# Layer 0: sums of squares dealt out by a transfer, the norms' key bias as a column of the keys, and its offset in one VectorE operation per kind

## The reference

```python
q = _ln(q, qln_w, qln_b)
k = _ln(k, kln_w, kln_b)
...
qx = _ln(qx, qxln_w, qxln_b)
kx = _ln(kx.reshape(b, sc, g, d), kxln_w, kxln_b)
...
core = _gqa(q, k, v).reshape(b, s, nh * d)
xout = _gqa(qx, kx, vx).reshape(b, s, nh * d)
cat = jnp.concatenate([core, xout], axis=-1)
catq = _div_clamp_fp8(cat, proj_smooth)
```

## Time and profile before

| | us |
|---|---|
| median of 3 runs | 1788.65 |
| lowest, highest | 1786.4, 1791.87 |
| span of the profiled execution | 1787.7 |

### The profile page before, as it was taken

How to read it: one execution, slowest core, us unless ns; L and a number is a source line. 1 busy time by engine, 2 the same in 40 slices (tenths; PEclk the granted TensorE clock), 3 DMA queues, 4 the chain that set the end, 5 groups by cost and what they waited for, 6 DMA issues and landing times. The chain is left out here.

```text
span 1787.7 us, 44278 instructions
## 1 busy us (share of the span) xinstructions
PE 1631.5 (91%) x16245; PEld 1038.3 (58%) x16438; DVE 1474.9 (83%) x3476; ACT 1386.3 (78%) x2365; POOL 1367.9 (77%) x1171
## 2 busy tenths in 40 slices
PE   3389999999999999999999999997898999999997
PEld 1256776777767767777777777765454333333332
DVE  8889999999999989999999999998896765645422
ACT  4287887888878777887887888775234999999996
POOL 3557787887878888888888888887897998979500
PEclk8599999999999999999999999999899999999999
DMA  4268999999899979999999999998523222222100
GB/s 168 93 130 180 184 187 193 198 194 190 189 199 184 200 150 198 191 231 184 195 195 192 217 213 190 194 186 160 171 42 110 41 44 75 43 37 43 31 14 13
DMA packets 603176, 261.42 MB, mean 146 GB/s; under 512 B 568784, under 2 KB 575952, under 8 KB 601552
## 3 DMA queue, kind: packets, MB, share of 16 engines
q1 hardware_dynamic: 602960, 258.57, 70.1%
HBM read 99.15 MB, written 17.28 MB: 65 GB/s over the span
## 5 line engine op out<-in xcount | busy, mean ns | idle before, releaser
L1800 PE MATMUL pv<-PT,VV 128*128 128x256 bf16 (+1 forms) x2880 | 340.9, 275 | 9.2 <-DMA PT<-PB 9.2
L1780 PE MATMUL score<-KK,QT 128*128 128x512 bf16 (+2 forms) x1795 | 315.6, 318 | 32.6 <-DVE mxp L1249 24.3
L2370 POOL TENSOR_TENSOR l_rr<-l_rr,mhalf 128x32 f32<-128x32 f32 (+1 forms) x60 | 332.8, 5546 | 5.0
L1521 ACT ACTIVATE PB<-S,rsum 128x1024 bf16<-128x1024 f32 (+1 forms) x256 | 246.2, 988 | 105.3 <-DVE rsum L1281 101.1
L1800 PEld LDWEIGHTS pv<-PT,VV 128*128 128x128 bf16 (+1 forms) x2880 | 280.7, 99 | 76.4 <-issue 35.2
L1272 DVE SCALAR_TENSOR_TENSOR PB<-S,rsum,PB 128x1024 bf16<-128x1024 f32 (+1 forms) x256 | 318.7, 1246 | 2.7 <-ACT PB L1521 2.6
L1780 PEld LDWEIGHTS score<-KK,QT 128*128 128x128 bf16 x1920 | 159.9, 98 | 164.5 <-DVE mxp L1249 32.3
L1511 ACT ACTIVATE S<-S,nmx 128x1601 f32<-128x1601 f32 x128 | 209.7, 1638 | 28.3 <-DVE nmx L1263 27.8
L2636 ACT ACTIVATE P<-score 128x1024 f32<-128x1024 f32 x196 | 199.4, 1063 | 12.7 <-PE score L2728 6.0
L1076 POOL TENSOR_SCALAR S<-S,rsum 128x256 f32<-128x256 f32 x128 | 122.0, 954 | 86.1 <-DVE rsum L1281 86.1
L2748 PE MATMUL pv<-P,V 128*9 128x256 f32 (+1 forms) x2288 | 153.9, 384 | 3.8 <-DVE pv L2174 2.4
(11 more groups left out here) (275 smaller groups left out, 3686.7 us busy)
## 6 DMA issues: line engine op xcount, KB each, us to landing
x<-rs_d SPq DMA_DIRECT2D x16, 936.0 KB, 7.6
rsb<-rs_d SPq DMA_DIRECT2D x16, 936.0 KB, 6.0
wsb<-w_split SPq DMA_DIRECT2D x46, 256.0 KB, 4.7
wsb<-w_split SPq DMA_DIRECT2D x23, 512.0 KB, 5.2
wpr<-in_wprojT SPq DMA_DIRECT2D x23, 512.0 KB, 3.9
context_d<-stage SPq DMA_DIRECT2D x16, 400.2 KB, 3.7
l_ctx<-context_d SPq DMA_DIRECT2D x4, 1601.0 KB, 8.1
rawh<-in_w_all SPq DMA_DIRECT2D x12, 512.0 KB, 5.6
```

Source lines behind the costliest of these rows:

```text
L1521: e.activation(m.PB[n % 2][:, 2 * a:a + b], m.S32[n % 2][:, a:b], ACT.Copy, scale=m.rsum[n % 2][:, 1:2]).then_inc(s["p_hi"], 1)
L1780: i = e.matmul(m.score[:, at:at + b - a], qt[:, kind, qp, q * P:(q + 1) * P], kk[:, kp, a:b], start=(k == 0), stop=(k == 2))
L1800: i = e.matmul(m.pv[:, at:at + 256], vv[0:rows, v, t, :], m.PT[k % 2][0:rows, turned(c, a), :], start=(c == first and r == 0), stop=(c == ...
L2370: e.tensor_tensor(rr, rr, m.mhalf[0:rows, 0:NH1], ALU.pow).then_inc(s["l1_rr"], 1)
```

## The change

The four rows of sums (now 480 wide) are copied by ACT with the epsilon added, and a transfer from SBUF to SBUF (`turn_sums`) deals them out to 128 partitions of 15. GpSimd takes the power of a 128x15 tile, and `row_out` writes that tile as it is to `rs_d`. The two sorts of PE transposes, VectorE's `squares_out` and ACT's `norms_out` go, and with them the slot ST (left empty) and RS. The key bias over sqrt(128) becomes one more column of each kind of keys (high and low part), written by VectorE in the first two turns alone, so that the scores' matmuls are 66 and 257 columns wide for 65 and 256 and bring q.b along in `m.score`. The eight matmuls, `m.kb` and `cb` go. `offset` becomes one scalar_tensor_tensor per kind, with q.b read from PSUM. Since it reads PSUM, `scores(n, 1)` now waits for `negmax` of the tile before. On GpSimd `key_norm` moves behind `split_self(4*it + 1)`. A few small tiles move in SBUF.

```diff
-SQG, SQT = 4, 4
-SQW = (KC + SQG * SQT - 1) // (SQG * SQT)
+SQG = 4
+SQC = (KC + P - 1) // P
+SQW = P * SQC // SQG
...
-         ("V2",), ("RS", "V3"), ("PR",))
+SLOTS = (("Q0",), ("K0",), ("K1",), ("TQ0",), ("K2",), ("K3",), ("Q1",), ("SS",), ("V0",), (), ("V1",), ("TQ1",), ("V2",),
+         ("V3",), ("PR",))
...
+    def turn_sums(it):
+        e.wait_ge(s["sums_out"], it + 1)
+        if it:
+            e.wait_ge(s["kr_pow"], it)
+        e.dma_start(m.ssc[:, :], m.sqs[0:SQG * R:R, :].rearrange("j (r c) -> j r c", c=SQC)).then_inc(s["sums_in"], 16)
...
     def row_out(it):
-        e.wait_ge(s["rst_out"], it + 1)
+        e.wait_ge(s["kr_pow"], it + 1)
...
-        e.dma_start(m.rs_d[it % 2], m.rsr[0:SQN, 0:SQW]).then_inc(s["rs_row"], 16)
+        e.dma_start(m.rs_d[it % 2], m.rr[:, :]).then_inc(s["rs_row"], 16)
...
     def key_norm(it):
-        e.wait_ge(s["ssq_out"], it + 1)
+        e.wait_ge(s["sums_in"], 16 * (it + 1))
...
+        e.tensor_tensor(m.rr[:, :], m.ssc[:, :], m.mhalf[:, 0:SQC], ALU.pow).then_inc(s["kr_pow"], 1)
...
+        split_self(4 * it + 1)
         key_norm(it + 1)
         if it == -1:
             pool_round_end(e, m, s, 5)
-        split_self(4 * it + 1)
...
     def offset(n):
-        e.tensor_tensor(m.mxc[par][:, :], m.mx[par][:, :], c, ALU.add).then_inc(s["maxed"], 1)
-        e.wait_ge(s["maxed"], n + 1)
         if n >= 2:
             e.wait_ge(s["exp_s"], n - 1)
-        e.tensor_tensor(m.nmx[par][:, :], c, m.mxc[par][:, :], ALU.subtract).then_inc(s["negmax"], 1)
+        for kind in range(2):
+            c, top = m.score[:, BIAS[kind]:BIAS[kind] + 1], m.mx[par][:, kind:kind + 1]
+            i = e.scalar_tensor_tensor(m.nmx[par][:, kind:kind + 1], top, c, c, ALU.add, ALU.subtract, reverse1=True)
+        i.then_inc(s["negmax"], 1)
...
-        e.copy(m.sqs[:, :], bank_of(m, "SS")[:, 0:SQT * SQW]).then_inc(s["sums_out"], 1)
+        e.activation(m.sqs[:, :], bank_of(m, "SS")[:, 0:SQW], ACT.Copy, bias=D * EPS5).then_inc(s["sums_out"], 1)
...
-        if n:
-            e.wait_ge(s["mm"], 3 * (n - 1) + (1, 3)[half])
+        if n and half == 0:
+            e.wait_ge(s["mm"], 3 * (n - 1) + 1)
+        elif n:
+            e.wait_ge(s["negmax"], n)
...
-            (1, 1024, 1536, 1024), (1, 1536, SC, 1536), (0, SC, KC, SELF0))
+            (1, 1024, 1536, 1024), (1, 1536, SC + 1, 1536), (0, SC + 1, KCOLS, SELF0))
```

More of the change, by code:

```diff
@@ L29 @@
 KC = SC + S
+KCOLS = KC + 2
 KTILES = KT + TB
@@ L894, in wait_bank @@
         it, at = it - 1, at + len(SLOTS)
-    if SLOTS[at] == ("PR",) and 0 <= it < LAG:
+    if not SLOTS[at] or SLOTS[at] == ("PR",) and 0 <= it < LAG:
         at -= 3
@@ L1655, in squares @@
         if it == 0:
-            e.wait_ge(s["p_pad"], 2)
-        w = SQT * SQW
+            e.wait_ge(s["p_pad"], 1)
         for j in range(SQG):
-            r = e.matmul(bank[j * R:(j + 1) * R, 0:w], m.ones[:, :], m.sq[:, j * w:(j + 1) * w], start=True, stop=True,
-                         skip_group_check=True)
-        r.then_inc(s["pa_full"], 1)
-    def turn_squares(it):
-        if not it < NGB:
-            return
-        bank = bank_of(m, "ST")
-        wait_bank(e, s, it, "ST")
-        e.wait_ge(s["sums_out"], it + 1)
-        for t in range(SQT):
-            r = e.transpose(bank[0:SQW, t * P:(t + 1) * P], m.sqs[:, t * SQW:(t + 1) * SQW], m.ident[:, :])
+            r = e.matmul(bank[j * R:(j + 1) * R, 0:SQW], m.ones[:, :], m.sq[:, j * SQW:(j + 1) * SQW], start=True,
+                         stop=True, skip_group_check=True)
         r.then_inc(s["pa_full"], 1)
@@ L1698, in values @@
                              start=(n == 0), stop=(n == 3))
-            e.wait_ge(s["q_hi"], 2 * it + 2)
-            for kind, q in itertools.product(range(2), range(NQ)):
-                at = 3 * D + kind * NQ + q
-                e.matmul(bank[:, at:at + 1], m.QT[it % 2][:, kind, 0, q * P:(q + 1) * P], m.kb[:, kind:kind + 1],
-                         start=True, stop=True)
             for n, (ic, part, w) in enumerate(inner):
```

117 lines of the change are left out of this document (39 added, 78 removed).

## The result

The changed kernel takes **1831.2 us** (median; 1827.0 to 1832.72, four runs) against 1787.53 for the kernel before in the same runs: a ratio of 1.0236, interval 1.0211 to 1.026. It is 44 us slower. I had forecast 24 us faster, and the time lies outside the range.

A forecast was written before the change was run, and what follows sets the result against it. PE was taken to bound the second part (35.0 us a turn), a PE-VectorE ring the first (36.9), the norms' row close behind. Gains 18 + 5 + 1 = 24 us; 1787.7 - 24 + 0.95 = 1764.6, range 1747 to 1790.

The forecast's parts named there:

- PE in the second part: Last 15 measured turns of layer 0's loop: PE's instruction stream sets the pace, 35.0 us a turn, falling to 34.0.
- the ring: First 15 measured turns: PE from released scores to values, then VectorE to `mxp`; 36.9 us a turn, 1.2 saved.
- The two operations behind the power: GpSimd's queue after the norms' power: two operations come some 2 us later, with no reader that soon; no cost counted.
- The row's chain: From `scaled(4*it, 0)` through sums, power, write and broadcast of the norms' row: 34.6 us a turn, the second part's new bound.
- The offset: VectorE's two tiny operations per offset become one: pair at 0.2 us, gain counted as 0.5 us a turn (bounds 0 and 1.0).
- PE's part: Dropped transposes and one-column matmuls: PE's work falls 0.95 to 1.1 us a turn in the second part, 0.72 in the first.
- a delay of 2 us there is absorbed: SP's queue behind `row_out`, which waits for the power: SP idles some 10 us a turn, so no cost.
- My 5.4: Sums' transfer behind SP's two transposes of probabilities: sums arrive about 5.4 us after standing ready, plus a 0.4 us tail.
- the rival in which PE's gain is kept: Transfer lands with the transposes, so PE's whole gain in the second part counts: 37 us saved, 1751.6; chance 0.15.
- `negmax`: Rival: PE's scores wait 0.2 to 0.5 us a turn for VectorE's offset in the second part; about 1773, chance 0.05.
- The row comes late: Rival: transfer tail and row write take x us longer; 1804 at x = 1.5, 1830 at 2.5; chance 0.15.
- my 18: First part's forecast gain: 0.72 for transposes plus 0.5 for the offset, 1.2 us a turn over 15 turns.

The follow-up runs named there:

- `pow_late`: Changed kernel with GpSimd's power moved two operations later in its queue, behind add_magnitudes and the second query_low: 1823.2 us.
- `ts_early`: Changed kernel with SP issuing the dealing transfer one place earlier, between the two transposes of probabilities instead of behind both: 1781.68 us.
- `bias`: Kernel before with the key-bias column and the one-operation offset alone, the sums going their old way: 1807.46 us.
- `bias_one`: `bias` plus an unread VectorE operation with one SBUF operand behind the offset of query tile 3: 1786.54 us.
- `bias_hold`: `bias` plus an unread VectorE addition of two SBUF operands behind the offset of query tile 3: 1786.39 us.
- `early_two`: `ts_early` plus two unread VectorE additions of two SBUF operands behind the offset of query tile 3: 1766.03 us.
- `early_swap`: `ts_early` with VectorE adding the projection ahead of p_lo(4*it + 2, 0) instead of behind it: 1765.61 us.
- `early_hold`: `ts_early` plus one unread VectorE addition of two SBUF operands behind the offset of query tile 3: 1792.32 us.
- the exchange: VectorE adds the projection ahead of p_lo(4*it + 2, 0) instead of behind it: alone on the changed kernel 1825.92 us, on the kernel before 1810.08.

## Why the prediction was wrong

*What bounds.* PE in the second part, the ring in the first, the row close behind: this held for the kernel before, but it was not all. A fourth chain was as close and I didn't see it: GpSimd's queue up to `a_nm`, then `kn`, then PE's transposes of queries. The list of waits didn't show it, since nobody waits for one who comes just in time; the timeline did. GpSimd took up `a_nm` 0.45 us after VectorE's `a_mv` in all 14 turns, so it was already the late one, and what was left until ACT's `kn` was 0.42 us in the mean.

*"The two operations behind the power come some 2 us later; they have no reader that soon."* **This is the step that failed first.** Not two but all operations behind the power come later, and the reader is `kn`. The price is a ring that feeds itself: power late, `a_nm` late, sums late, power late. I counted 0; the power starts 5.5 us after the sums where it was 1.5, GpSimd's wait there is 39.0 us in 490 for 27.4, and ACT's for `a_nm` 28.0 for 0.7. `pow_late` shifts the wait from GpSimd to the row, and `ts_early`, which shortens the delay itself, brings GpSimd's wait down to 7.3 us and VectorE's for the row from 23.0 to 7.1: the two share one delay.

*The row's chain.* What it has behind the sums was right in sum. Sums to power 5.47 us (5.4 + 0.4 forecast); power to the issue of the write 3.03 (2.7 + 0.1); from there to the row's landing 8.21 (1.7 + 7.1). That is 16.7 for 17.4. The term in front was the one mis-sized: `scaled(4*it, 0)` to the sums took 20.19 us and not 17.2. 20.19 + 16.7 + 0.16 of rest is the turn, 37.1. So VectorE waits for the row, as I said it would, but the row is late because of what lies ahead of the sums, which I had made 0.7 us shorter and took over otherwise from a trace in which GpSimd was in time.

*The offset.* In the turn shown the pair holds VectorE's queue for 0.25 us, near the 0.2 that I took. Counted as a gain of 0.5 us a turn, it brought none in the first part (`bias` 37.06 for 36.92) and cost 1.25 us in the second. I had noted that VectorE's next two-operand operation might wait for the same operation of GpSimd, and halved the gain for it. I applied the rule of the Trainium skill (SBUF — State Buffer, Who interferes with whom) to VectorE's duration only. The same section says that issue order decides who blocks; this case's trace agrees, with 1.28 and 2.26 us for one and the same `catq`. The side I didn't price was GpSimd's, and its bound can't be read from the duration of any row: it is a place in an order.

*PE's part.* The four transposes, eight matmuls and the transpose back seem to be worth something: with the order restored, `bias_one` and `bias_hold`, which drop only the eight matmuls, run the second part at 34.8 for 35.03, and `early_two` at 34.37, with PE busy for 486.7 of 490 us. I had forecast 34.4 to 34.6 for that part, and 35.7 for the first, where the best here are 35.93 and 36.09.

*SP.* That SP waits idly and "a delay of 2 us there is absorbed" holds for the loads: no wait of 660:1150 names one. But for the new transfer SP was the obstacle: it was issued 2.0 to 3.6 us after the sums, since the second transpose ahead of it was still being issued, and the power started at least 2.1 us after that issue, 2.8 in the mean. My 5.4 came from the landing of the transposes and was right in size by luck. The difference matters: read as landing time it "cannot be shortened", as I wrote against the rival in which PE's gain is kept; read as a place in the queue it goes away by moving one line.

*The rivals.* `negmax` doesn't bind: no wait of PE in 660:1150 names `nmx`. "The row comes late" gave 1804 at x = 1.5 and 1830 at x = 2.5. The measured second-part turn is 34.6 + 2.5, the first part's 35.2 + 2.5, and the time is its number. That is luck, since the mechanism isn't its: tail and write are not longer (the write lands after 1.4 us in the median, the whole behind the sums is below the forecast). That none of my cases had GpSimd as the late one is why 0.15 stood on the side that came.

*The total.* 1764.6 is what `early_swap` (1765.6) and `early_two` (1766.0) reach, the change with most of both side effects taken away. This is agreement in size, not in parts: in `early_swap` the first part gains 12 us for my 18, the second 2 for my 5, and 5 us lie behind the last sums where I had put 1 (its profiled execution, 1770.4 us; the median is 5 us lower).

*Open.* Why `p_lo` wins in `early_hold` and `catq` in `bias_one` and `bias_hold`, with the same 0.02 us between their recorded starts, isn't settled. GpSimd's subtraction ahead of them goes with it in every turn: in the nine kernels with such meetings it takes 0.67 or 0.68 us in all 116 in which `catq` is first, and 0.69 or 0.70 in all 24 in which `p_lo` is (five more in `early_swap`, where the subtraction is itself held up for a microsecond, left aside). What makes it so isn't known. How the 43 us of the changed kernel divide isn't a number, but the late transfer is the larger part: repairing it gives 49 us, while the exchange gives 5 by itself, with ranges that overlap, and 16 on top of the repaired transfer.

## What to carry to other kernels

When an edit takes a wait away, ask who was let through by it: list the operations of the other engine that become ready at that moment, and what stands behind them in that engine's queue. A delay at one operation is a delay of its whole queue, so follow the queue to each semaphore that someone else waits for, and measure in the timeline how long it is signalled before it is used: that is the margin, and where it is small the list of waits shows nothing. And a short transfer on which an engine waits goes ahead of the long ones in the issuing queue, or into another queue.
